# Attention with its scores turned: softmax weights stationary, row sums from columns of ones, casts shared between three engines

## The chip, the cores and the metric

The kernel runs on one core of a Trainium2 chip, in one launch. The metric is the device time of that launch in microseconds (us); less is better. Four compute engines with queues of their own take part: TensorE (PE; its weight loads are listed apart as PEld), VectorE (DVE), ScalarE (ACT) and GpSimd (POOL); SyncE (SP) issues the DMAs. Each engine works through its instructions in order and waits on semaphores for the others.

## What is computed

One layer of three blocks on 256 tokens of width 512, each added to a residual: cross attention over 4096 context rows and the 256 tokens themselves, a state-space block, and a mixture of 32 experts (6 used per token) with a shared expert. The change touches the first. Cut to what matters:

```
q = rope(rms_norm(x_norm @ wq))            # 16 heads of 128, 256 queries
k = [rms_norm(ctx @ wk_ctx), rope(rms_norm(x_norm @ wk))]   # 4 kv heads, 4096 + 256 keys
v = [ctx @ wv_ctx, x_norm @ wv]
s = q @ k.T / sqrt(128)                    # the last 256 keys are causal
w = softmax(s, axis=keys)
x = x + (w @ v).reshape(256, 2048) @ wo
```

Four heads share one kv head. Everything is float32. The kernel splits an operand into a high part (a cast to fp32r) and a low part (the rest) and sums three products: high by high, high by low, low by high.

## The kernel before, in words

The context is projected first (`project`, to about 234 us), K and V tiles with their high and low parts go to DRAM (`k_spill`, `v_spill`), and come back for one kv head at a time as `kT` (2 x 4352 keys) and `vN`. Then the attention stage runs head by head, in 17 steps a head (`NPAIR`; one step is 256 keys). The step numbers, the order of score chunks and their banks come from `Plan`: a score chunk is 128 queries by 512 keys, and scores are made one head ahead of the weights.

- `score` (L577): the queries (`qT`) are stationary and 512 keys of `kT` move, three products a chunk. `evict` (L1033, L1037, VectorE) writes the chunk to `scores` in SBUF and takes its row maximum; `maximum` makes `neg_max`.
- `exponential` (L1545, ScalarE): exp of 1024 keys for 128 queries with the row's maximum as bias; the row sums come along (`sums`), are inverted (L1052) and spread over partitions (`spread_sums`, L645).
- `turn_weights` (L593, TensorE): four transposes a step bring the weights to keys by queries in one of three banks. ScalarE casts them to the high part in the ring `pT` of four tiles (L1574), VectorE subtracts it for the low part (L1114).
- `weigh` (L616, L618), three steps behind (`LAG`): V is stationary and the weights move; 512 columns hold high and low parts side by side, then 256 columns for V's low part: four products a step. The output comes out as head width by queries, in two halves that `finish_head` adds and scales (L1060 to L1064, VectorE), casts (L1551, ScalarE) and splits (L1823, GpSimd).
- After the last head the output projection: 2 x 16 x 3 products of 512 columns (L673). While it runs, `w_xa` and `w_z` for the next block are loaded (issued by SyncE once the last value product is done), `w_xa` is split, VectorE adds the residual (L1133) and normalises (L937, `un`), and TensorE goes on with `w_z` (L686).

GpSimd's splits stand elsewhere: L1828 (`wo_lo`) at the end of the attention. L847, L849 and L741 are products of the later blocks, L493 a helper for products of several of them.

## Time and profile before

| | us |
|---|---|
| median of 3 runs | 1041.34 |
| lowest, highest | 1040.83, 1042.22 |
| the profiled execution, first to last instruction | 1040.1 |
| TensorE busy in it | 1034.4 |
| VectorE, ScalarE, GpSimd busy | 780.6, 610.6, 182.9 |

The profile is of one execution. Its span leaves out what lies around the instructions, so it stands 1.2 us under the median. Busy times of TensorE are modelled for pipelined matmuls: what a matmul costs is read from start to start. An instruction of VectorE or ScalarE overlaps the next by up to 0.1 us.

### The profile page before, as it was taken

How to read it: one execution, taken by the hardware profiler on the slowest of the kernel's cores; microseconds unless marked ns; L12 is line 12 of the kernel's file. 1: busy time of each engine (PE TensorE's matmuls, PEld its weight loads, DVE VectorE, ACT ScalarE, POOL GpSimd, SP SyncE). 2: the span in 40 equal slices, each digit the busy share in tenths (PEclk: the TensorE clock that was granted, in tenths of full speed). 3: DMA queues.
4: the chain of work that ended last, by engine and by line, in shares of the span. 5: the costliest groups of instructions: out<-in, count | busy, mean ns of one | idle time of the engine just before them, and what ended most of it. 6: DMA issues, size and time to landing. Idle time of an engine off the chain costs nothing.

```text
span 1040.1 us, 15687 instructions
## 1 busy us (share of the span) xinstructions
PE 1034.4 (99%) x5837; PEld 890.9 (86%) x5837; DVE 780.6 (75%) x1674; ACT 610.6 (59%) x1106; POOL 182.9 (18%) x200
## 2 busy tenths in 40 slices
PE   9999999999999999999999999999999999999998
PEld 8888888888888888888888888889887988888887
DVE  6856777649777777777877777877669977777775
ACT  5434343335765566665556665569469566666664
POOL 4544434330000000000000000002201132222221
...
GB/s 278 231 183 292 205 243 187 130 317 317 11 1 163 56 127 1 2 172 82 92 1 1 172 122 56 1 1 184 202 163 1 152 295 224 191 184 191 192 162 21
DMA packets 64299, 145.76 MB, mean 140 GB/s; under 512 B 3904, under 2 KB 42720, under 8 KB 62688
## 3 DMA queue, kind: packets, MB, share of 16 engines
...
q8 instruction: 46, 0.75, 0.3%
...
## 4 chain that ended last, share of the span: by engine, by line
PE 97%; DVE 2%; ACT 1%; DMA 1%; issue 0%; SPq 0%
PE bank L511 17%; PE bank L577 17%; PE bank L493 12%; PE bank L616 12%; PE bank L593 11%; PE bank L877 9%; PE bank L618 6%; PE bank L879 4%; PE bank L673 2%; PE bank L686 1%; PE bank L520 1%; DVE scores L1033 1%; PE bank L741 1%; DMA w_ctx_raw<-in_w_ctx 1%; PE bank L847 1%; PE bank L545 0%
## 5 line engine op out<-in xcount | busy, mean ns | idle before, releaser
L1114 DVE TENSOR_TENSOR pT<-bank,pT 128x512 fp32r<-128x512 f32 x272 | 184.8, 689 | 101.8 <-ACT pT L1574 100.0
L1574 ACT CAST pT<-bank 128x512 fp32r<-128x512 f32 x272 | 156.0, 593 | 141.9 <-PE bank L593 138.8
L616 PE MATMUL bank<-pT,vN 128*128 128x512 f32 (+1 forms) x544 | 225.7, 422 | 0.0
L577 PE MATMUL bank<-kT,qT_hi 128*128 128x512 f32 (+2 forms) x576 | 214.4, 391 | 0.7 <-DVE scores L1033 0.7
L1033 DVE TENSOR_SCALAR_CACHE_REDUCE scores<-bank 128x512 f32<-128x512 f32 x256 | 172.6, 686 | 1.6
L593 PE MATMUL bank<-ident,scores 128*128 128x128 f32 x1072 | 161.3, 272 | 0.1
L1545 ACT ACTIVATE scores<-scores,neg_max 128x1024 f32<-128x1024 f32 (+2 forms) x128 | 154.0, 1204 | 6.2 <-DVE neg_max L1045 6.2
L618 PE MATMUL bank<-pT,vN 128*128 128x256 f32 (+1 forms) x544 | 152.5, 280 | 0.0
L511 PE MATMUL bank<-w_ctx_hi,ctx_hl 128*128 128x512 f32 x512 | 144.5, 394 | 0.4 <-ACT w_ctx_hi L1511 0.4
L877 PE MATMUL bank<-fT_parts,e_hl 128*128 128x512 f32 x392 | 139.9, 394 | 0.0
L593 PEld LDWEIGHTS bank<-ident,scores 128*128 128x128 f32 x1072 | 127.1, 140 | 11.5 <-DVE pT L1114 0.6
L577 PEld LDWEIGHTS bank<-kT,qT_hi 128*128 128x128 f32 x576 | 108.3, 189 | 16.3 <-DVE scores L1033 1.2
L618 PEld LDWEIGHTS bank<-pT,vN 128*128 128x128 f32 x544 | 102.6, 189 | 15.6
L511 PEld LDWEIGHTS bank<-w_ctx_hi,ctx_hl 128*128 128x128 f32 x512 | 94.9, 188 | 19.9 <-ACT w_ctx_hi L1511 0.9
L879 PE MATMUL bank<-fT_parts,e_hl 128*128 128x256 f32 x392 | 110.1, 281 | 0.0
L577 PE MATMUL bank<-kT,qT_lo 128*128 128x512 f32 (+2 forms) x288 | 109.8, 381 | 0.0
L616 PEld LDWEIGHTS bank<-pT,vN 128*128 128x128 f32 x544 | 103.1, 190 | 3.8
L1692 ACT CAST e_hl<-e_raw 128x1536 fp32r<-128x1536 f32 x51 | 75.5, 1483 | 38.5 <-PE bank L493 38.5
L1823 POOL TENSOR_TENSOR outT<-head_out,outT 128x256 fp32r<-128x256 f32 x16 | 11.8, 739 | 475.1 <-ACT outT L1551 475.1
L1463 ACT ACTIVATE k_stage<-bank,k_w 128x512 fp32r<-128x512 f32 x32 | 22.1, 690 | 119.6 <-PE bank L520 119.6
L877 PEld LDWEIGHTS bank<-fT_parts,e_hl 128*128 128x128 f32 x392 | 73.5, 188 | 17.7 <-DVE e_hl L1266 0.4
L1266 DVE TENSOR_TENSOR e_hl<-e_raw,e_hl 128x1536 fp32r<-128x1536 f32 x49 | 85.9, 1753 | 0.0
...
## 6 DMA issues: line engine op xcount, KB each, us to landing
...
k_spill<-k_stage SPq DMA_DIRECT2D x16, 1024.0 KB, 5.6
v_spill<-v_stage SPq DMA_DIRECT2D x16, 1024.0 KB, 8.2
vN<-v_spill SPq DMA_DIRECT2D x16, 1024.0 KB, 5.5
kT<-k_spill SPq DMA_DIRECT2D x15, 1024.0 KB, 5.5
...
w_raw<-in_w_qkv SPq DMA_DIRECT2D x6, 1024.0 KB, 5.0
wo_sb<-in_wo SPq DMA_DIRECT2D x4, 1024.0 KB, 7.7
```

Source lines behind the costliest of these rows:

```text
L493: done = e.matmul(dst, lhs(a), rhs(w), start=first and m == 0, stop=last and m == 2)
L511: done = e.matmul(bank[2 * j + z][:, :], ctx_hl[z][:, a, k, :], w_ctx[w][:, k, j, :], start=m < 2, stop=m >= len(order) - 2)
L577: done = e.matmul(bank[b][:, 0:n], qT[a][:, h, qt * P:(qt + 1) * P], kT[:, w, lo:lo + n], start=m == 0, stop=m == 2)
L593: done = e.transpose(bank[tb][:, i * P:(i + 1) * P], s_buf[2 * z + qt][:, kt * P:(kt + 1) * P], ident[:, :])
L616: e.matmul(halves[:, :, q0:L], vN[:, 0, kt, :], ring[:, :, i * L + q0:(i + 1) * L], start=kt == 0, stop=False)
L618: done = e.matmul(halves[:, 0, q0:L], vN[:, 1, kt, :], ring[:, 0, i * L + q0:(i + 1) * L], start=False, stop=kt == KTILES - 2)
L877: e.matmul(bank[b][:, :].rearrange("p (x t) -> p x t", x=2), w[:, 0, m, k * P:(k + 1) * P], fT_parts[:, :, k, :], start=k == 0, stop=False)
L879: done = e.matmul(bank[b][:, 0:L], w[:, 1, m, k * P:(k + 1) * P], fT_parts[:, 0, k, :], start=False, stop=k == KD - 1)
L1033: e.tensor_scalar(s_buf[row][:, lo:lo + CH], bank[b][:, 0:CH], 1.0, None, ALU.mult, ALU.max, accum_out=chunk_max[row][:, c:c + 1]).then_in ...
L1114: e.tensor_tensor(ring[:, 1, :], bank[tb][:, :], ring[:, 0, :], ALU.subtract).then_inc(p_lo, 1)
L1545: e.activation(s_buf[row][:, lo:hi], s_buf[row][:, lo:hi], ACT.Exp, bias=neg_max[row][:, 0:1], scale=SCALE, accum_out=sums[z][:, qt, i:i + ...
L1574: e.copy(ring[:, 0, :], bank[tb][:, :]).then_inc(p_hi, 1)
```

## The change

The attention stage is written anew; the stages before and behind keep their instructions. A step is still 256 keys of one head, 17 a head, and the projection of the context runs on as before.

- *Scores turned.* Keys (128 of `kT`) are stationary and 256 queries move: six products a step, keys on partitions. So the weights need no transposes.
- *Maxima.* They now run over partitions. ScalarE copies each step's scores to SBUF (`take_scores`), VectorE keeps a running maximum over steps (`running_max`), folds it (`fold_max`), TensorE transposes it, VectorE reduces (`reduce_rows`), TensorE spreads it back over partitions (`spread_max`), and VectorE subtracts it from the scores in SBUF, 1024 columns at a time (`subtract_max`). ScalarE's exponentials carry no bias and no sums.
- *High and low parts.* The weights lie in SBUF. 12 of a head's 17 high parts are cast by ScalarE and 5 by VectorE (`HI_ON_DVE`), in the last 25 steps all by ScalarE; every low part is GpSimd's, in the last 25 steps every other one VectorE's.
- *Values.* The weights are stationary, 128 queries at a time, and V moves: 12 products a step of 130, 128 and 130 columns. `vH` has two columns of ones behind the 128 of the head, whose products are the row sums; `finish_head` scales by their reciprocal, and two transposes turn the output (`turn_out`).
- *Order.* Scores run 25 steps ahead (`LEAD`), values 3 behind the casts (`LAG`). 15 heads of one half of the output projection stand between the last value steps, and six of the other half ahead of the last head's transposes.

The core of the diff:

```diff
+LEAD = NG + 8
 LAG = 3
+SUB_AHEAD, EXP_AHEAD = 4, 2
+HI_ON_POOL = ()
+HI_ON_DVE = (1, 4, 7, 10, 13)
+WO_STEP = 252
+WO_PRODUCTS = 254
...
+            def score(s):
...
+                if s >= len(SCORE_BANKS):
+                    wait_score_bank(pe, s - len(SCORE_BANKS))
...
+                    for m, (a, w) in enumerate(PRODUCTS):
+                        done = e.matmul(dst, kT[:, w, kt * P:(kt + 1) * P], qT[a][:, h, q0:L], start=m == 0, stop=m == 2)
...
+            def weigh(n):
...
+                wait_lo(pe, n)
...
+                        e.matmul(bank[b][:, out:out + HV], ring[:, 0, at:at + P], vH[:, kt, :], start=kt == 0 and qt == 0, stop=False)
+                        yield
+                        e.matmul(bank[b][:, out:out + HD], ring[:, 0, at:at + P], vL[:, kt, :], start=False, stop=False)
+                        yield
+                        done = e.matmul(bank[b][:, out:out + HV], ring[:, 1, at:at + P], vH[:, kt, :], start=False, stop=kt == KTILES - 1)
...
-                    done = e.transpose(bank[tb][:, i * P:(i + 1) * P], s_buf[2 * z + qt][:, kt * P:(kt + 1) * P], ident[:, :])
...
+            for s in range(NH * NG + LEAD + LAG + 1):
...
+                n = s - LEAD
+                in_turns(score(s), weigh(n - LAG))
+                h, k = divmod(s - NG, NG)
+                if h in range(NH):
+                    if k == 1:
+                        turn_max(h)
+                    if k == 3:
+                        spread_max(h)
+                h, k = divmod(n - NG, NG)
+                if k == LAG + 1 and h in range(H15):
+                    turn_out(h)
+                if WO_PRODUCTS <= n < WO_PRODUCTS + H15:
+                    project_out(0, n - WO_PRODUCTS)
+
+            for h in range(6):
+                project_out(1, h)
+            turn_out(H15)
+            project_out(0, H15)
+            for h in range(6, NH):
+                if h == H15 - 1:
+                    pe.wait_ge(ln_out, 3)
+                    wait_score_bank_at_end(pe, 6)
+                    turn_rows(2, 0, un)
+                project_out(1, h)
...
+                    e.tensor_tensor(run_max[:, :], src[:, :], run_max[:, :], ALU.max).then_inc(maxed, 1)
...
+                    e.tensor_tensor(rows, rows, top.unsqueeze(1).to_broadcast([P, 4, L]), ALU.subtract).then_inc(subbed, 1)
...
+                e.tensor_copy(pT[n % NPT][:, 0, 0:width(g)], weights_of(n)).then_inc(p_hi["dve"], 1)
...
+            for s in range(NH * NG + LEAD):
+                n = s - LEAD
...
+                if n in plan.hi["act"]:
+                    high_of_weights(n)
+                take_scores(s)
+                for h, j in quads_at(n + EXP_AHEAD):
+                    exponential(h, j)
...
+                e.tensor_tensor(ring[:, 1], weights_of(n), ring[:, 0], ALU.subtract).then_inc(p_lo["pool"], 1)
...
-                e.dma_start(vN[:, :, lo:hi, :].bitcast(F32).rearrange("p l t d -> p l (t d)"),
-                            v_spill[g][:, :, lo:hi, :].rearrange("l p t d -> p l (t d)")).then_inc(v_in[i], 16)
+                for part, dst in enumerate((vH[:, lo:hi, 0:HD], vL[:, lo:hi, :])):
+                    e.dma_start(dst.bitcast(F32), v_spill[g, part][:, lo:hi, :]).then_inc(v_in[i], 16)
```

TensorE, in the last head of before, where no scores are left: transposes, then the value products of an earlier step (`bank` is a PSUM bank, the number behind a name its buffer).

```order
L593 MATMUL bank<-ident,scores_116 128x128 [waits p_lo]
L593 MATMUL bank<-ident,scores_117 128x128
L593 MATMUL bank<-ident,scores_116 128x128
L593 MATMUL bank<-ident,scores_117 128x128
L616 MATMUL bank<-pT_119,vN 128x512
L618 MATMUL bank<-pT_119,vN 128x256
L616 MATMUL bank<-pT_119,vN 128x512
L618 MATMUL bank<-pT_119,vN 128x256
L593 MATMUL bank<-ident,scores_116 128x128 [waits p_lo]
```

TensorE in the middle of a head after, the first 12 of a step's 18 products (operands are printed moving or stationary in either order; `pT` and `kT` are stationary here).

```order
L598 MATMUL bank<-qT_hi,kT 128x256 [waits maxed]
L619 MATMUL bank<-vH,pT_117 128x130 [waits p_lo_pool]
L621 MATMUL bank<-vL,pT_117 128x128
L598 MATMUL bank<-qT_hi,kT 128x256
L623 MATMUL bank<-vH,pT_117 128x130
L619 MATMUL bank<-vH,pT_117 128x130
L598 MATMUL bank<-qT_lo,kT 128x256
L621 MATMUL bank<-vL,pT_117 128x128
L623 MATMUL bank<-vH,pT_117 128x130
L598 MATMUL bank<-qT_hi,kT 128x256
L619 MATMUL bank<-vH,pT_117 128x130
L621 MATMUL bank<-vL,pT_117 128x128
```

The transposes are gone, and between two score products of 256 columns stand two value products of 128 or 130.

VectorE in the middle of a head, before: low parts of the weights and evictions in turns.

```order
L1114 TENSOR_TENSOR pT_119<-bank,pT_119 128x512 [waits p_hi]
L1033 TENSOR_SCALAR scores_117,chunk_max_125<-bank 128x512 [waits scored]
L1114 TENSOR_TENSOR pT_120<-bank,pT_120 128x512 [waits p_hi]
L1033 TENSOR_SCALAR scores_117,chunk_max_125<-bank 128x512 [waits scored] x2
L1114 TENSOR_TENSOR pT_121<-bank,pT_121 128x512 [waits p_hi]
L1033 TENSOR_SCALAR scores_117,chunk_max_125<-bank 128x512 [waits scored]
L1114 TENSOR_TENSOR pT_118<-bank,pT_118 128x512 [waits p_hi]
L1033 TENSOR_SCALAR scores_117,chunk_max_125<-bank 128x512 [waits scored]
```

VectorE after, around the fourth step of a head (L1065 running maximum, L1108 and L1112 the head's end, L1085 subtraction, L1096 cast).

```order
L1065 TENSOR_TENSOR run_max<-bank,run_max 128x512 [waits maxed,taken,scored]
L1108 RECIPROCAL rden_125<-bank 128x2 [waits pv]
L1112 TENSOR_TENSOR head_out_129<-bank,rden_125 128x256 [waits out_turned,ho]
L1065 TENSOR_TENSOR run_max<-bank,run_max 128x512 [waits maxed,taken,scored]
L1085 TENSOR_TENSOR weights_115<-weights_115,bank 128x1024
L1096 CAST pT_119<-weights_115 128x512 [waits pv,expd]
L1065 TENSOR_TENSOR run_max<-bank,run_max 128x512 [waits maxed,taken,scored]
L1116 TENSOR_TENSOR outT_127<-bank,outT_126 128x256 [waits oT_hi]
```

The low parts have left VectorE; a cast of this step stands behind a maximum, which waits for the scores of a group 25 steps ahead, and behind a subtraction.

GpSimd in the same place, after: one low part a step; before, it had one instruction a head there (L1823).

```order
L1887 TENSOR_TENSOR pT_117<-weights_116,pT_117 128x512 [waits pv,p_hi_act]
L1887 TENSOR_TENSOR pT_118<-weights_116,pT_118 128x512 [waits pv,p_hi_dve]
L1887 TENSOR_TENSOR pT_119<-weights_116,pT_119 128x512 [waits pv,p_hi_act]
L1887 TENSOR_TENSOR pT_120<-weights_116,pT_120 128x512 [waits pv,p_hi_act]
L1887 TENSOR_TENSOR pT_117<-weights_116,pT_117 128x512 [waits pv,p_hi_dve]
```

TensorE at the end of the attention, before: last value products, then the whole output projection.

```order
L616 MATMUL bank<-pT_121,vN 128x2x128 [waits p_lo]
L618 MATMUL bank<-pT_121,vN 128x128
L616 MATMUL bank<-pT_121,vN 128x512
L618 MATMUL bank<-pT_121,vN 128x256
L673 MATMUL bank<-wo_hi,outT_142 128x512 [waits oT_lo,wo_lo_dve,maxed]
L673 MATMUL bank<-wo_lo,outT_142 128x512
L673 MATMUL bank<-wo_hi,outT_143 128x512
L673 MATMUL bank<-wo_hi,outT_142 128x512 [waits oT_lo,wo_lo_pool]
```

TensorE there after. 45 products of the projection stand further up, between the value steps, and 51 follow.

```order
L619 MATMUL bank<-vH,pT_120 128x130
L621 MATMUL bank<-vL,pT_120 128x128
L623 MATMUL bank<-vH,pT_120 128x130
L671 MATMUL bank<-wo_hi,outT_126 128x512
L671 MATMUL bank<-wo_lo,outT_126 128x512
L671 MATMUL bank<-wo_hi,outT_127 128x512
L671 MATMUL bank<-wo_hi,outT_126 128x512
L671 MATMUL bank<-wo_lo,outT_126 128x512
```

## Rows read from the trace of the kernel before

**Rows 1.** Page: span; engine busy us (share) xinstructions; chain that ended last, by engine.
```profile
span 1040.1 us, 15687 instructions
...
PE 1034.4 (99%) x5837; PEld 890.9 (86%) x5837; DVE 780.6 (75%) x1674; ACT 610.6 (59%) x1106; POOL 182.9 (18%) x200
...
PE 97%; DVE 2%; ACT 1%; DMA 1%; issue 0%; SPq 0%
```

**Rows 2.** Stretches view, all engines, inside attention: busy us (xinstructions), clock, DMA share, GB/s.
```profile
300.00:650.00 350.00, 350.00 (x2152) 310.52 (x2151) 269.54 (x696) 219.10 (x397) 8.13 (x11) 1.00 0.23 78
```

**Rows 3.** Timeline, TensorE (start us, us, engine line op names form): attention's first and last products, w_z's.
```profile
234.37 0.71 PE L577 MATMUL bank<-kT,qT_hi 128*128 128x512 f32 x2
...
734.78 0.28 PE L618 MATMUL bank<-pT,vN 128*128 128x256 f32 x1
...
757.71 1.88 PE L686 MATMUL bank<-w_z,uT 128*128 128x512 f32 x4
```

**Rows 4.** Chain of waits in order of time (start us, us, engine, tile, line xcount).
```profile
752.29 5.58 PE bank L673 x24
...
766.87 14.29 PE bank L493 x120
...
804.79 3.52 PE bank L741 x32
```

**Rows 5.** Timeline, TensorE, 256 and 128 columns in turns.
```profile
818.23 0.33 PE L847 MATMUL bank<-fT_parts,e_hl 128*128 128x256 f32 x1
818.39 0.22 PE L849 MATMUL bank<-fT_parts,e_hl 128*128 128x128 f32 x1
818.46 0.33 PE L847 MATMUL bank<-fT_parts,e_hl 128*128 128x256 f32 x1
...
819.82 0.33 PE L847 MATMUL bank<-fT_parts,e_hl 128*128 128x256 f32 x1
```

**Rows 6.** Timeline, TensorE, a value step without scores in the last head.
```profile
713.40 0.60 PE L593 MATMUL bank<-ident,scores 128*128 128x128 f32 x4
...
714.54 0.60 PE L593 MATMUL bank<-ident,scores 128*128 128x128 f32 x4
```

**Rows 7.** Groups by line and form (busy us, mean ns | idle before).
```profile
L593 PE MATMUL bank<-ident,scores 128*128 128x128 f32 x1072 | 161.3, 272 | 0.1
```

**Rows 8.** Timeline, ScalarE: exponential, two casts from PSUM, three from SBUF.
```profile
710.33 1.17 ACT L1545 ACTIVATE scores<-scores,neg_max 128x1024 f32<-128x1024 f32 x1
...
713.56 1.10 ACT L1574 CAST pT<-bank 128x512 fp32r<-128x512 f32 x2
...
736.84 1.66 ACT L1556 CAST wo_hi<-wo_sb 128x512 fp32r<-128x512 f32 x3
```

**Rows 9.** Timeline, VectorE (evictions, splits) and GpSimd (splits).
```profile
243.79 0.68 DVE L1033 TENSOR_SCALAR_CACHE_REDUCE scores<-bank 128x512 f32<-128x512 f32 x1
...
244.40 0.69 DVE L1033 TENSOR_SCALAR_CACHE_REDUCE scores<-bank 128x512 f32<-128x512 f32 x1
...
720.92 1.29 POOL L1828 TENSOR_TENSOR wo_lo<-wo_sb,wo_hi 128x512 fp32r<-128x512 f32 x1 [0.79 <-ACT wo_hi L1556]
...
737.71 3.00 POOL L1828 TENSOR_TENSOR wo_lo<-wo_sb,wo_hi 128x512 fp32r<-128x512 f32 x2
...
739.59 2.20 DVE L1129 TENSOR_TENSOR w_xb_lo<-w_xb,wx_hi 128x1024 fp32r<-128x1024 f32 x1
744.00 4.63 DVE L1129 TENSOR_TENSOR w_xa_lo<-w_xa,wx_hi 128x1024 fp32r<-128x1024 f32 x4 [2.20 <-ACT wx_hi L1595]
```

**Rows 10.** Timeline, VectorE behind the attention: residual and normalised rows.
```profile
748.54 0.68 DVE L1133 TENSOR_TENSOR x_sb<-x_sb,bank 128x512 f32<-128x512 f32 x1
...
751.03 0.55 DVE L937 TENSOR_SCALAR un<-x_sb,moments,rstd 128x512 f32<-128x512 f32 x1 [0.67 <-POOL rstd L1787]
```

**Rows 11.** Timeline, VectorE: last instruction of the key stage.
```profile
238.04 0.69 DVE L964 TENSOR_TENSOR k_normed<-bank,k_rs 128x512 f32<-128x512 f32 x1
```

**Rows 12.** Page, DMA issues: KB each, median us to landing.
```profile
vN<-v_spill SPq DMA_DIRECT2D x16, 1024.0 KB, 5.5
```

751 lines of the change are left out of this document (374 added, 377 removed).

## The prediction

> **What bounds the kernel now.** I read the page's busy shares and the chain that ended last first, then the timeline of TensorE inside the attention stage, then those of the engines beside it. TensorE is busy 1034.4 of 1040.1 us and holds 97% of the chain [rows 1]; between 300 and 650 us it has no idle time at all, while VectorE is busy 269.5 and ScalarE 219.1 of 350 us, GpSimd 8.1 us, and the granted clock is 1.00, its 2.4 GHz level [rows 2]. So a wait on another engine is not what costs time; the cost of the matmuls, start to start, is. The attention stage runs from 234.37 us to 735.06 us (734.78 + 0.28, the end of the last value product) [rows 3]: 500.7 us.
>
> What the reader must see in the rows of TensorE is the spacing, not the duration (durations overlap). A 512-column product takes 0.233 us (24 in 5.58 us), a 256-column one 0.119 us (120 in 14.29 us), and a 64-column one still 0.110 us (32 in 3.52 us) [rows 4]. Where 256 and 128 columns alternate, seven pairs take 819.82 - 818.23 = 1.59 us, 0.227 us a pair; were the streams alone to count, 384 columns would take 0.227 x 384/512 of a 512-column price, 0.175 us [rows 4, 5]. So small products have a floor near 0.110 us, that of the weight load that each one brings along. A value step without scores lasts 714.54 - 713.40 = 1.14 us: 2 x (0.233 + 0.119) = 0.70 for four value products, and 0.44 for four transposes, 0.110 each [rows 4, 6]. Check of these prices on the kernel before, per head: scores 48 x 0.233 + 3 x 0.119 + 3 x 0.110 = 11.9; values 34 x (0.233 + 0.119) - 0.13 = 11.8; transposes of the weights 67 x 0.110 = 7.4; spreading the sums 0.2. That is 31.3 us, 501 us for 16 heads, against 500.7 in the trace. The prices hold.
>
> **What the change removes and adds on TensorE.** Removed: 1072 transposes [rows 7], 16 x 7.4 = 118 us, and the four value products of a step. The scores keep their columns but come as 256-column products: two 256s (0.238) stand for one 512 (0.233). The values turn round: the weights are stationary and the values move, so a step has 12 products of 128 or 130 columns. Their streams are no longer than before (1552 columns against 1536), but each brings a load: 12 x 0.110 = 1.32 us where 0.70 + 0.44 = 1.14 us stood. The diff shows where twelve come from: the high part meets vH and vL in two products with the same stationary tile, and the output projection of before has the same pattern (outT high with wo_hi, then wo_lo), with no product cheaper for it: 24 in 5.58 us [rows 4].
> Per head: 17 x 18 = 306 products less 3 unseen and with 3 score products halved: 99 of 256 columns, 105 + 99 small ones. 99 pairs x 0.227 = 22.5, 105 x 0.110 = 11.6, together **34.0 us**, 2.00 us a step. For 16 heads 544.4 us. Around it: 94 transposes for maxima and outputs x 0.110 = 10.3; the last keys' four, 0.4; and 15 of the 32 output-projection groups now run inside the tail, 15 x 3 x 0.233 = 10.5. Stream up to the last value product: 565.6 us.
>
> A page speaks against that floor. The Trainium skill, "TensorE: Matmul & The Clock Gate", section "Back-to-back issue gap", gives about 81 ns a product for a sustained stream of load and matmul with 128 columns; the same page, section "LDWEIGHTS (loading the stationary operand)", gives columns over 1.2 GHz, 107 ns. The trace agrees with the second (0.110 us); by the first, which no row here shows, a step would take about 1.7 us, and that is a rival below.
>
> **The other engines: does one of them pass 34.0 us a head?** ScalarE: 16 copies of scores at 0.50 (two casts from PSUM end after 1.08), 12 casts at 0.53 (three in 1.66), 8 exponentials of 1024 at 1.05 (1.17, of which 0.1 lies under the next), a short one and the output: 16 x 0.50 + 12 x 0.53 + 8 x 1.05 + 0.7 = 23.5 us [rows 8]. GpSimd, nearly idle before, gets the low part of every step: 17 x 1.29 = 21.9 us [rows 9]. VectorE: 15 running maxima, each waiting for its predecessor, at 0.69 + 0.04 = 0.73; the masked group 1.3 (three instructions of 384, 256 and 128 columns, an estimate from 0.69 for 512); folding and reducing 0.8; 8 subtractions of 1024 columns at 1.16 (four splits in 4.63) and two short ones 0.6 [rows 9]; the head's end 1.0; and 5 casts, for which the trace has no row: at most 0.69, the two-input size, at least half of 0.55, and taken as 0.55, the row of one input and 512 columns [rows 10]. That is 11.0 + 1.3 + 0.8 + 9.9 + 1.0 + 2.8 = 26.8 us. All lie under TensorE; it stays the bound, and this work is hidden in the mean.
>
> **Where it is not hidden.** (a) *VectorE's casts.* A cast of step n stands in VectorE's queue behind the running maximum of the score group s = n + 25, and in 3 of 5 cases (10, 13, 4) behind a subtraction too. From the start of TensorE's step s: the last score product, 16th of the 18, starts at 15 x 0.111 = 1.67 and is done at 1.95; ScalarE's copy to 2.57; maximum issued 2.60; subtraction 3.2 to 4.4; cast to 4.9; GpSimd 1.29, to 6.2. TensorE wants the result after three steps and one product, 6.1. Late by 0.1, and one load is then bare: 0.25 us. 14 heads x 3 + 1 = 43 such casts x 0.25 = 11 us; between nothing (a fast cast) and 0.5 each, 21 us. The other casts have a second to spare each, and ScalarE's casts more. (b) *Lead-in.* Steps 0 to 27 hold scores only, 0.71 us each; VectorE enters at 238.7 (238.04 + 0.69) [rows 11] and must do 22 maxima (16.1), the masked group (1.3), the last keys' rest (0.75), fold and reduce (0.8) and two subtractions (2.4) before TensorE may write the bank of step 28: 260.1 us. TensorE alone would be there at 234.4 + 19.9 + 1.1 = 255.4. **5 us**, between 2 and 9. In the kernel before an eviction took 0.61 us (243.79 to 244.40) [rows 9] for 0.70 us of products, and nothing was lost.
> (c) *After the last value product.* Before, TensorE took 757.71 - 735.06 = 22.65 us from there to the first product with w_z, all of it output projection [rows 3]. Its cover was long enough for w_xa's loads and splits, which the change leaves where they are: they wait for the last value product, and VectorE adds the residual (748.54) and has the normalised rows at 751.58, 16.5 us after it [rows 10]. Now only 12.1 us of projection is left, so TensorE waits: 16.5 + 0.44 for four transposes + 1.4 for two heads = 18.4 us. Against 22.65 that gives back 4.3, of the 10.5 us moved forward; 6 us are lost.
> (d) K and V tiles are requested at the same points of a head as before and have over 12 steps (24 us) to land, where 5.5 us were enough [rows 12]. The values' high half is now written in shorter pieces; at double the time it still lands early: nothing.
>
> **Sum.** 565.6 + 11 + 5 = 581.6, less 500.7, is +80.9; less 4.3, +76.6. Behind that the programs are the same. The profiled execution would be 1040.1 + 76.6 = 1116.7 us, and the median lies 1.2 us above the span: **1118 us**.
>
> **Rivals.** *The loads hide* (the other side, faster). If a small product cost only its stream, as the 0.07 us from a 128-column start to the next might suggest [rows 5], TensorE would need 17 x (6 x 0.119 + 12 x 0.06) = 24.4 us a head, VectorE's 26.8 would bound, and against the 505 us of before (500.7 + 4.3) stand 16 x 26.8 + 21.2 + 5 = 455: -50, 991 us. It decides from 0.090 us a small product: then a head takes 99 x 0.117 + 204 x 0.090 = 30 us, and the change is even. For it: a queue that loads ahead. Against it: the pairs at 0.227 and 64 columns at 0.110 [rows 4, 5]. 4%. By the 81 ns of the Trainium skill's page just named a head would take 28 us and the kernel about 1012 us; no row shows such spacing.
> *VectorE becomes the bound through GpSimd.* GpSimd now works two thirds of the time, and a VectorE instruction that reads two SBUF tiles stretches beside it: 2.20 us at 739.59, under GpSimd's 3.00, against 4.63/4 = 1.2 when alone [rows 9]. Casts, fold and masked maxima are 8 such a head; blocked by a whole 1.29 each, VectorE needs 26.8 + 10.3 = 37.1 us a head against TensorE's 34.7 (34.0 and six transposes), and the time is 1118 + 16 x 2.4 - 11 = 1145 us. It decides from 1.0 us lost each. 12%. The Trainium skill, "SBUF — State Buffer", section "Who interferes with whom", calls the shared pair an exclusive lock; maxima and subtractions have one input in PSUM and stand outside it, which leaves only the 8 named.
> *Nothing stalls.* A fast cast and a short lead-in: 565.6 + 2 - 505 = +63, 1104 us. Part of the forecast's own range.
> *A clock that falls*, since streams fill only half of TensorE's time: over 1200 us. Stretches of small products show 1.00. 2%.
>
> **How the numbers follow.** Forecast (TensorE bound by loads, small stalls) 80%: 1098 to 1135. VectorE 12%, 1135 to 1155; faster 4%; far slower (the clock, or an unseen wait in every step) 4%. The range 1096 to 1146 leaves out under 2 in 10. What a measurement can tell from no change is 0.2%, 2 us: faster 4%, same 1%, slower 95%.
>
> **What would show it.** Right: 18 products a step in 2.00 us, small ones 0.110 apart, no L593 transposes of weights, TensorE over 95% busy and the heads 34.7 to 35.5 us apart; short idle times before the step after a VectorE cast, released by GpSimd; a wait of 6 us before the transposes of un. Wrong: spacing under 0.09 us; VectorE busy all through a head with TensorE waiting for running maxima; a granted clock under 1.00.

## The result, and the profile after it

| kernel | time, us | span, us | granted clock of the span |
|---|---|---|---|
| before, four executions | 1040.8 to 1042.2 | 1040.1 | 1.00 |
| changed, two executions | 1166.2, 1166.6 | 1164.5, 1164.9 | 0.96 |
| changed, two executions | 1575.3 (profiled), 1598.4 | 1573.5, 1596.7 | 0.687, 0.676 |

The times of the changed kernel are of two kinds, and that is the result: what parts them is the granted clock of TensorE. The comparison uses the lower kind, 1.120 times the kernel before (1.118 to 1.122). The forecast was 1118 us, with 1146 as its upper end.

The profile after is of an execution of 1575 us. First the page: the span, TensorE's busy time, its busy share and its granted clock in 40 slices, and the chain by engine.

```profile
span 1573.5 us, 20080 instructions
...
PE 1556.4 (99%) x7725; PEld 1466.7 (93%) x7725; DVE 793.9 (50%) x1304; ACT 684.5 (43%) x1153; POOL 494.3 (31%) x445
...
PE   9999998999999999999999999999999989999999
...
PEclk9999999555555555555555555555555699999999
...
PE 97%; DVE 1%; DMA 1%; ACT 0%; issue 0%; POOL 0%; SPq 0%; DVEq 0%
```

Beside [rows 1] nothing looks amiss but the clock: TensorE is 99% busy and holds 97% of the chain. The granted clock reads 5, the 1.2 GHz level, in 24 slices. The stretches view (us; TensorE busy, its weight loads, VectorE, ScalarE, GpSimd, each with its count; clock; DMA share; GB/s) shows where it falls, stays and returns:

```profile
262.00:266.00 4.00, 2.61 (x19) 2.30 (x19) 3.87 (x7) 3.99 (x7) 1.33 (x2) 1.00 1.01 300
266.00:270.00 4.00, 3.70 (x26) 3.70 (x27) 2.23 (x4) 1.73 (x4) 2.74 (x3) 0.81 0.04 13
270.00:274.00 4.00, 4.00 (x21) 4.00 (x21) 1.83 (x3) 1.46 (x3) 2.78 (x3) 0.50 0.00 0
300.00:1200.00 900.00, 900.00 (x4238) 900.00 (x4236) 333.89 (x519) 328.17 (x524) 289.62 (x232) 0.50 0.10 31
1240.00:1244.00 4.00, 4.00 (x18) 3.81 (x17) 1.57 (x5) 1.79 (x4) 0.65 (x1) 0.50 0.02 4
1244.00:1248.00 4.00, 4.00 (x29) 3.75 (x29) 2.52 (x5) 1.71 (x4) 1.87 (x2) 0.91 0.00 0
```

At 0.50 the stream is the same, only slower: 900 us without a gap, where [rows 2] has 350, the other engines a third busy. The price of a product rises almost twofold. Timeline of TensorE, at 1.00 and at 0.50:

```profile
262.63 0.34 PE L598 MATMUL bank<-qT_hi,kT 128*128 128x256 f32 x1
...
262.97 0.33 PE L598 MATMUL bank<-qT_lo,kT 128*128 128x256 f32 x1
...
600.24 0.52 PE L598 MATMUL bank<-qT_hi,kT 128*128 128x256 f32 x1
...
600.88 0.52 PE L598 MATMUL bank<-qT_hi,kT 128*128 128x256 f32 x1
```

From one 256-column product to the next three products start (the 256-column one and two value products): 262.97 - 262.63 = 0.34 us at 1.00 (the prediction had 0.337), 600.88 - 600.24 = 0.64 us at 0.50. So 0.113 and 0.213 us a product: the floor of small products in [rows 4, 5] moves with the clock.

Now the last thing that TensorE did before the fall. Timelines of TensorE, VectorE and GpSimd:

```profile
266.30 0.33 PE L619 MATMUL bank<-vH,pT 128*128 128x130 f32 x1 [1.64 <-POOL pT L1887]
```

```profile
262.74 1.21 DVE L1085 TENSOR_TENSOR weights<-weights,bank 128x1024 f32<-128x1024 f32 x1
263.87 0.69 DVE L1065 TENSOR_TENSOR run_max<-bank,run_max 128x512 f32<-128x512 f32 x1
264.47 0.42 DVE L1096 CAST pT<-weights 128x512 fp32r<-128x512 f32 x1
```

```profile
261.02 1.28 POOL L1887 TENSOR_TENSOR pT<-weights,pT 128x512 fp32r<-128x512 f32 x1 [22.45 <-ACT pT L1611]
264.97 3.77 POOL L1887 TENSOR_TENSOR pT<-weights,pT 128x512 fp32r<-128x512 f32 x3 [2.67 <-DVE pT L1096]
```

The first value products stand at 262.35 us. Two microseconds on, TensorE waits 1.64 us for GpSimd's low part of step 1, GpSimd had waited for VectorE's cast (264.47), and that cast stood behind a subtraction and a running maximum. It is the only cast of the attention for which TensorE waits so. Some two us after the wait the clock is 0.50, and the waits in the lead-in before it (0.3 to 1.2 us) had not moved it. It comes back at 1244.7 us. In between one head takes 65.66 us (transposes of head_out at 464.74 and 530.40).

**What the fall costs.** From 268.5 to 1244.7 us, 976 us are spent at 0.50. A head at 1.00 takes 35.43 us (shown below). 976 x (1 - 35.43/65.66) = 449 us, and 1573.5 - 449 = 1124 us would be left. In the two executions near 1166 us a mean clock of 0.96 means some 93 us at 0.50, and 93 x 0.46 = 43 us; that leaves 1122. Both are near the forecast span of 1116.7 us. The experiments had to show that this reckoning is right, and what makes the clock fall and stay.

### The profile page after: what moved, and what is told of

Same layout as the page of the kernel before. It is cut to its first block, busy times and chain, and to the rows that moved or that the text cites. A ratio compares the mean times of both kernels' runs of the same rounds, so it can differ in the third digit from the quotient of the medians.

```text
span 1573.5 us, 20080 instructions
## 1 busy us (share of the span) xinstructions
PE 1556.4 (99%) x7725; PEld 1466.7 (93%) x7725; DVE 793.9 (50%) x1304; ACT 684.5 (43%) x1153; POOL 494.3 (31%) x445
## 4 chain that ended last, share of the span: by engine, by line
PE 97%; DVE 1%; DMA 1%; ACT 0%; issue 0%; POOL 0%; SPq 0%; DVEq 0%
PE bank L598 29%; PE bank L524 11%; PE bank L623 11%; PE bank L621 11%; PE bank L619 11%; PE bank L506 8%; PE bank L905 6%; PE bank L907 3%; PE bank L671 1%; PE bank L713 1%; PE bank L533 1%; DVE run_max L1065 1%; DMA w_xa<-in_w_in 0%; PE bank L642 0%; PE bank L769 0%; PE bank L650 0%
## 5 line engine op out<-in xcount | busy, mean ns | idle before, releaser
L1887 POOL TENSOR_TENSOR pT<-weights,pT 128x512 fp32r<-128x512 f32 (+1 forms) x259 | 323.6, 1266 | 694.1 <-DVE pT L1096 532.0
L598 PE MATMUL bank<-qT_hi,kT 128*128 128x256 f32 (+1 forms) x1088 | 526.2, 494 | 2.9 <-DVE run_max L1065 1.7
L1065 DVE TENSOR_TENSOR run_max<-bank,run_max 128x512 f32<-128x512 f32 x224 | 154.9, 691 | 480.5 <-ACT weights L1601 364.1
L619 PE MATMUL bank<-vH,pT 128*128 128x130 f32 x1072 | 384.9, 359 | 1.6 <-POOL pT L1887 1.6
L623 PE MATMUL bank<-vH,pT 128*128 128x130 f32 x1072 | 386.3, 360 | 0.0
L621 PE MATMUL bank<-vL,pT 128*128 128x128 f32 x1072 | 386.2, 360 | 0.0
L619 PEld LDWEIGHTS bank<-vH,pT 128*128 128x128 f32 x1072 | 346.1, 323 | 2.9 <-POOL pT L1887 1.8
L621 PEld LDWEIGHTS bank<-vL,pT 128*128 128x128 f32 x1072 | 346.2, 323 | 1.0
L623 PEld LDWEIGHTS bank<-vH,pT 128*128 128x128 f32 x1072 | 346.3, 323 | 0.0
L598 PEld LDWEIGHTS bank<-qT_hi,kT 128*128 128x128 f32 x1088 | 341.0, 317 | 4.3 <-DVE run_max L1065 2.5
L598 PE MATMUL bank<-qT_lo,kT 128*128 128x256 f32 (+1 forms) x544 | 267.6, 492 | 0.0
L598 PEld LDWEIGHTS bank<-qT_lo,kT 128*128 128x128 f32 x544 | 172.4, 317 | 0.0
L1085 DVE TENSOR_TENSOR weights<-weights,bank 128x1024 f32<-128x1024 f32 x128 | 154.9, 1210 | 3.9 <-PE bank L650 3.9
```

Of the source, the lines that this page charges most:

```text
L598: done = e.matmul(dst, kT[:, w, kt * P:(kt + 1) * P], qT[a][:, h, q0:L], start=m == 0, stop=m == 2)
L619: e.matmul(bank[b][:, out:out + HV], ring[:, 0, at:at + P], vH[:, kt, :], start=kt == 0 and qt == 0, stop=False)
L621: e.matmul(bank[b][:, out:out + HD], ring[:, 0, at:at + P], vL[:, kt, :], start=False, stop=False)
L623: done = e.matmul(bank[b][:, out:out + HV], ring[:, 1, at:at + P], vH[:, kt, :], start=False, stop=kt == KTILES - 1)
L1065: e.tensor_tensor(run_max[:, :], src[:, :], run_max[:, :], ALU.max).then_inc(maxed, 1)
L1085: e.tensor_tensor(rows, rows, top.unsqueeze(1).to_broadcast([P, 4, L]), ALU.subtract).then_inc(subbed, 1)
```

## Experiments: is it the stream, or the wait?

Theory A: the short products alone let the clock fall. Theory B: the waits of the lead-in (the steps with scores only, before the first value product) do. Each kernel below was executed four or six times, and one of its executions was traced. The edits are shown shortened.

**The same kernel again.**

> The changed kernel once more, unaltered, for the spread of its times and for a trace in which the clock is high most of the time. The one trace so far (span 1573.5 us) has a granted clock of 0.50 from 270 to 1244 us, while TensorE is busy without a gap; its products stand 0.213 us apart there and 0.113 us apart before and after. Both theories (A: the stream of short products, each behind its own weight load, lets the clock fall; B: the waits of TensorE in the lead-in, steps 0 to 27, let it fall, and it then stays down) expect times of two kinds again, near 1166 and near 1575 to 1598 us, with little between. In an execution near 1166 us the mean clock is 0.96: I expect some 93 us (8% of 1165) at 0.50, and a step of 18 products in 2.03 us in all the rest. At 0.50 a step lasts 3.84 us, so 93 us there cost 93 x (1 - 2.03/3.84) = 44 us, and 1166 - 44 = 1122 us would be left for the kernel at full clock.

1165.3 us once, 1577.0 to 1598.6 us five times (clock 0.676 to 0.687). The profiled execution, 1598.0 us, was again of the long kind, with the same wait of 1.64 us (it ends at 265.97 us) and the fall behind it. Here the clock stayed at 0.50 until 1298 us, not 1244.7: that is what parts 1598 from 1577. No trace of an execution near 1166 us exists, so where its 93 us at 0.50 lie was not seen.

**Value products of 256 columns.**

```diff
-e.matmul(bank[b][:, out:out + HV], ring[:, 0, at:at + P], vH[:, kt, :], ...)
+e.matmul(dst, ring[:, 0, at:at + P], vH[:, two, 0:HD], ...)   # two key tiles, 256 columns
```

> The value products move 256 columns instead of 128 or 130, over two key tiles at once, into 256 columns of the bank; so the row sums are left out and the output is another. Loads, number of products, waits and everything on the other engines stay. By the spacing of 256-column products, 0.119 us, a step lasts 18 x 0.119 = 2.14 us instead of 2.03, 28 to 30 us more in all. Theory A (the clock falls because short products behind their own loads leave the streaming part of TensorE idle): granted clock 1.00 in every execution, all times near 1122 + 30 = 1152 us, below the 1166 us of the changed kernel although more is streamed. Theory B (waits in the lead-in): those waits are the same, so the clock falls as before and the times are of two kinds, near 1195 and above 1550 us.

1147.1 to 1148.1 us. Waits of TensorE, then the stretch in which the changed kernel falls, then the attention:

```profile
PE bank L620 <- POOL pT L1888: 1.6, 1, 1.6
```

```profile
262.00:266.00 4.00, 2.45 (x20) 2.24 (x19) 4.00 (x6) 3.63 (x7) 1.43 (x2) 1.00 0.90 268
266.00:270.00 4.00, 4.00 (x34) 4.00 (x35) 2.15 (x4) 2.00 (x3) 2.35 (x2) 1.00 0.03 8
300.00:700.00 400.00, 400.00 (x3368) 399.99 (x3368) 277.67 (x415) 259.49 (x414) 236.32 (x187) 1.00 0.20 65
```

The wait is there, 1.55 us long, and the clock stays at 1.00 (row sums and so the output are others in this kernel). More is streamed than in the changed kernel, and the time is lower than its best. Even a wait of 1.00 us in the last head (794.8 us) moves nothing here. Theory B alone falls.

**The lead-in filled.**

```diff
-for m, (a, w) in enumerate(PRODUCTS):
+twice = s < LEAD + LAG and i == 0
+for m, (a, w) in enumerate(PRODUCTS + PRODUCTS + PRODUCTS if twice else PRODUCTS):
```

> In steps 0 to 27, the lead-in in which TensorE has only scores, the three products of a step's first key tile are issued three times, the last of which leaves the result; so TensorE has 1.42 us of work a step there instead of 0.71, which covers its waits for running maxima. All else is the changed kernel. The lead-in takes 28 x 1.42 = 40 us instead of 28, +12 us. Theory B (the waits in the lead-in make the clock fall): granted clock 1.00 throughout, 1122 + 12 = 1134 us in every execution. Theory A (the short products of the steps themselves): the clock falls after the first value steps as before, times near 1178 and near 1590 us.

1157.1 to 1159.1 us, and 1176.3 once. The clock is 1.00 from 220 to 788 us, through 500 us of the very stream that the long executions ran at 0.50: theory A alone falls too. It falls at 789 us, right behind a wait of 1.31 us for both_max, in the last head's steps, which have value products only:

```profile
300.00:780.00 480.00, 479.75 (x4188) 477.29 (x4186) 345.13 (x514) 323.25 (x518) 288.44 (x230) 1.00 0.18 57
780.00:790.00 10.00, 8.69 (x76) 8.55 (x76) 8.41 (x13) 6.35 (x10) 7.34 (x6) 0.98 0.40 138
790.00:800.00 10.00, 10.00 (x50) 10.00 (x49) 5.33 (x8) 4.21 (x7) 2.55 (x2) 0.50 0.83 338
```

```profile
789.24 0.46 PE L643 MATMUL bank<-ident,both_max 128*128 128x128 f32 x2 [1.31 <-DVE both_max L1072]
```

**No casts on VectorE.**

```diff
-HI_ON_DVE = (1, 4, 7, 10, 13)
+HI_ON_DVE = ()
```

> The five casts of a head that VectorE makes go back to ScalarE, nothing else is changed. The prediction put their price at 11 us (0 to 21), as loads left bare behind late low parts. At full clock I expect 11 us less than the changed kernel, 1155 us against 1166; if the casts were covered, 1166. ScalarE has 23.5 + 5 x 0.53 = 26.2 us a head and stays under TensorE's 34. Theory A and B both expect times of two kinds here too, near 1155 to 1166 and above 1550 us; a third theory (C: the late weights, small waits in each head, pull the clock down) expects 1.00 and about 1111 us in all executions.

1149.5 to 1152.4 us. No wait for GpSimd, no fall at 266 us, though the lead-in has all its waits. But there are new ones inside the attention, 14 of 0.62 us and one of 1.06 us in the last head, 9.7 us together. The 14 leave the clock at 1.00; during the one of 1.06 us, at 781 us, it falls:

```profile
PE bank L642 <- DVE both_max L1071: 9.7, 15, 1.1
```

```profile
262.00:266.00 4.00, 4.00 (x36) 4.00 (x37) 3.87 (x5) 4.00 (x8) 3.01 (x3) 1.00 0.88 263
266.00:270.00 4.00, 4.00 (x38) 4.00 (x37) 3.20 (x4) 3.42 (x6) 3.60 (x4) 1.00 0.03 6
```

So a further theory, **D**: a wait of one to two us *inside* the stream of short products lets the clock fall, and the stream does not bring it back.

## Experiments: the wait as the cause

**One wait put in by hand**, in head 8 of the kernel with the filled lead-in.

```diff
+if (h, g) == (8, GAP_AT):        # GAP_AT = 1
+    pe.wait_ge(ho, 2 * h)
```

> The kernel with the filled lead-in (three times the products of a step's first key tile in steps 0 to 27), and in it one wait of TensorE put in by hand: before the second value step of head 8 it waits until VectorE has finished head 7, which comes some 2 to 3 us later by VectorE's queue. It stands in the middle of the attention stage, where K and V loads are light. Theory D (a wait of TensorE of one to two us amid the short products lets the clock fall, and the stream of short products, 63% of TensorE's time in columns, does not bring it back): granted clock 1.00 up to this wait, 0.50 from it to the end of the value steps, 8.9 heads at 17 x 3.84 instead of 17 x 2.04 us: +270 us, 1158 + 270 less the 20 us lost at the end anyway, about 1410 us. Theory A (the short products alone) has no place for a change here: 1160 us with the fall at 790 us only. Rival E (the fall comes where the DMA queues are full, as at 266 and at 787 us, with 0.93 to 1.00 of their time): no fall at this wait, 1161 us.

1348.9, 1374.2 and 1374.6 us; once 1180.7. The wait was 1.87 us at 563.78, and the clock is 0.54 in the stretch from 564 to 568 us, 0.50 until the output projection. Three of four: the wait makes a fall likely, not sure. The DMA queues were at 0.92 just then, so rival E (full queues) was open, and so was the last head:

**The last head's transposes later**, in the kernel without casts on VectorE.

```diff
-if k == 1:
+if k == (2 if h == H15 else 1):
     turn_max(h)
```

> VectorE's casts go to ScalarE as in the run before, and for the last head alone the transposes of the maxima are issued one step later (and their spreading one step later), so that TensorE does not wait 1.06 us for VectorE at 781 us. The loads of w_z and others that fill the DMA queues from 780 us on stay. Theory D: no fall at 782 us, the clock is 1.00 up to the wait for the last rows; the 40 us at 0.50 in the kernel without VectorE's casts cost 40 x (1 - 1.35/2.56) = 19 us, so 1150.3 - 19 = 1131 us. Rival E (full DMA queues): fall as before, 1150 us.

1142.6 to 1143.8 us, and 1166.2 once. The wait at 781 us is gone, and the clock stays 1.00 there, with the queues at 1.01. It falls ten us later instead, at about 792 us, behind a new wait of 1.93 us for wo_lo. The edit shifted the wait, and the fall went with it; the expected 1131 us did not come.

**The wait in head 9, where the DMA queues are idle**, again with the filled lead-in.

```diff
+if (h, g) == (9, 1):
+    pe.wait_ge(ho, 2 * h)
```

> As the kernel with the filled lead-in and one wait put in by hand, but the wait stands in head 9 instead of head 8, near 598 us, where the DMA queues are under 0.02 busy for 45 us around (in head 8 they were at 0.92). Theory D: the fall comes at this wait in some or most executions (in head 8 in 3 of 4), and lasts to the end of the value steps: 5.9 x 2 = some 25 to 30 us less than the runs with the wait in head 8, since one head of 34.9 us at full clock would take 65 at half: 1349 - 31 = 1318, 1374 - 31 = 1343 us. Rival E (full DMA queues are needed): no fall at 598 us in any execution, 1161 us.

1318.3, 1318.5, 1340.6 and 1340.9 us, the expected 1318 and 1343. The DMA share is 0.00 to 0.02 at the fall, which lasts 388 us, from 599 to 987. Rival E falls.

```profile
590.00:594.00 4.00, 4.00 (x37) 4.00 (x37) 2.79 (x4) 2.65 (x4) 0.93 (x1) 1.00 0.00 0
594.00:598.00 4.00, 2.41 (x22) 2.21 (x20) 2.92 (x6) 2.54 (x4) 3.77 (x3) 1.00 0.00 0
598.00:602.00 4.00, 3.72 (x20) 3.75 (x20) 0.14 (x1) 0.50 (x2) 0.00 (x0) 0.58 0.02 4
602.00:606.00 4.00, 4.00 (x21) 4.00 (x20) 2.15 (x3) 1.87 (x4) 1.59 (x2) 0.50 0.00 0
```

**One cast moved**, that of step 1 of head 0.

```diff
-"dve" if n < tail and g in HI_ON_DVE else "act"
+"dve" if 1 < n < tail and g in HI_ON_DVE else "act"
```

> The changed kernel, in which one single cast, that of the high part of step 1 of head 0, goes from VectorE to ScalarE; the other 74 of VectorE's casts stay. In the slow traces it is this step's low part for which TensorE waits 1.64 us at 264.3 us, the last wait before the clock falls. Theory D (a wait amid the short products lets the clock fall, the stream of short products keeps it down): this wait goes, and with it the long fall, in every or nearly every execution; times 1150 to 1166 us, a mean clock of 0.96 to 0.98, and a fall only near 782 us. Theory A (short products alone) and F (VectorE's casts in general, through late weights in every head): times of two kinds as before, 1166 and 1577 to 1598 us.

1141.7 to 1145.3 us in all four. One instruction of 0.42 us, moved to another engine, takes away 434 us of the usual time (medians 1577.5 and 1143.6). The changed kernel's best time lies 23 us above this one, and that is mostly something else: 1.6 us are the wait, and some 20 fit a longer fall in the last head (below), with 93 us at 0.50 where this kernel has 48. Its clock is 1.00 until 777 us; then it falls during the last head's wait (1.31 us), for 38 us. VectorE's other casts are worth keeping: this kernel is 6.7 us faster than the one without them, as the waits for both_max, from 230 to 900 us, come to 2.7 us instead of 10.8.

**No fall at the end either.** In addition 12 products of 512 columns, overwritten later, in front of the last head's transposes.

```diff
+if k == 1 and h == H15:
+    wait_score_bank(pe, NH * NG - len(SCORE_BANKS))
+    for _ in range(12):
+        e.matmul(bank[SCORE_BANKS[0]][:, :], vH[:, 0, 0:HD], vH[:, 0:4, 0:HD], start=True, stop=True)
     turn_max(h)
```

> The cast of step 1 of head 0 on ScalarE as before, and in front of the transposes of the last head's maxima 12 products of 512 columns whose results are overwritten (12 x 0.233 = 2.8 us), so that TensorE does not wait 1.31 us there; all else is the changed kernel. Theory D: granted clock 1.00 from the start to the wait for the last rows, 16 heads, and the time is that of the changed kernel at full clock: 1143.6, less 40 us at 0.50 x (1 - 1.35/2.56) = 19, plus 2.8 - 1.3 = 1.5, 1126 us; the forecast of 1118 came without the head's both_max waits and with 2.00 us a step. If the short products without scores lose the clock by themselves (value steps of 12 products of 128 columns, 48% in columns), the fall comes all the same and the time is near 1146 us.

1127.0 to 1127.8 us against 1126 expected. The clock is 1.00 up to the wait for `un`. This is the changed kernel as the prediction had reckoned it, 2.9 us of fill included (12 products from 774.68 to 777.57 us).

## Experiments: why it does not come back

**64 columns a value product**, in the kernel without casts on VectorE. It asks whether a shorter wait is enough where the products carry fewer columns; half of the values and the row sums are left out.

```diff
-e.matmul(bank[b][:, out:out + HV], ring[:, 0, at:at + P], vH[:, kt, :], ...)
+e.matmul(bank[b][:, out:out + 64], ring[:, 0, at:at + P], vH[:, kt, 0:64], ...)
```

> Without VectorE's casts, and each value product moves 64 columns instead of 128 or 130, into the first 64 columns; so half of the values and the row sums are left out, and the output is another. All loads, waits and other engines' work stay. If the load sets the pace (0.110 us with 64 columns as with 128, as the prediction took it), a step lasts 1.98 instead of 2.03 us: about 1140 us at the same clock, against 1150. The columns then fill 2304 of 4750 possible ones of a step, 48% against 63%. [...]

1348.9, 1407.3, 1467.3 and 1526.4 us: four falls, by the times in four different heads. In the trace the pace at 1.00 is that of the changed kernel (three products in 0.34 us), and six waits of 0.64 to 0.66 us do nothing before the one at 495 us, behind which the next product is at half pace. With 128 columns fourteen waits of 0.62 us did nothing. So fewer columns make a shorter wait enough, and chance has a part.

```profile
494.05 0.37 PE L598 MATMUL bank<-qT_lo,kT 128*128 128x256 f32 x1
...
495.19 0.66 PE L642 MATMUL bank<-ident,both_max 128*128 128x128 f32 x2 [0.64 <-DVE both_max L1071]
495.50 0.56 PE L598 MATMUL bank<-qT_hi,kT 128*128 128x256 f32 x1
495.86 0.26 PE L619 MATMUL bank<-vH,pT 128*128 128x64 f32 x1
```

**48 products of 512 columns in the middle** of the changed kernel.

```diff
+if s == 5 * NG + 8:
+    for _ in range(48):
+        e.matmul(bank[b][:, :], kT[:, 0, piece * PIECE:piece * PIECE + P], kT[:, 0, piece * PIECE:piece * PIECE + 512], start=True, stop=True)
```

> The changed kernel with 48 products of 512 columns (results overwritten) put in once, before the scores of step 8 of head 5, when TensorE is in step 65 of the 244 that hold scores and values. Theory D with its second half (at half clock the stream of short products does not bring the clock back, more columns would): in executions in which it fell at 266 us, the clock comes back to 1.00 with the burst, at about 266 + 65 x 3.84 = 516 us, and stays there until the end of the scores: 65 x 1.8 = 117 us lost instead of some 410 to 430, 1166 + 117 + 11 = 1294 us in place of 1577 to 1598. In executions in which it did not fall, 1177 us. If the clock cannot come back amid the stage at all (it is held down for a time of its own): 1588 to 1610 us.

Twice 1156 us, four times 1253.3 to 1270.5 (expected 1294). The burst starts at about 513 us; the stretch from 512 to 516 us has 0.77, the next 1.00, and it stays so to the last head (900 us). The clock can come back amid the stage, and it holds once it is up.

In the last head 15 value steps carry three 512-column products of the output projection each. Fourteen traces run them at 0.50, from the first on. In ten the clock is back in the sixth such step, some 21 us after the first (first at 1223.9, back at 1244.7; in the kernel with one cast moved 793.4 and 814.4). In four (the second trace of the changed kernel, 64 columns, and two kernels below) it stays at 0.50 through all 15 and comes back 3 to 5 us after the projection's products stand alone. Here is one of the four (the last of the kernels with score products in a row, below), where the first such product stands at 805.1 us:

```profile
794.00:826.00 32.00, 32.00 (x135) 30.26 (x134) 14.65 (x22) 13.20 (x21) 10.14 (x10) 0.50 0.13 50
826.00:874.00 48.00, 48.00 (x200) 45.40 (x199) 10.92 (x19) 12.50 (x19) 12.38 (x10) 0.50 0.00 0
```

Between the two traces of the changed kernel this makes 1598 us of 1575, and it would explain the step of 18 to 26 us that other kernels show too (1318 and 1341, 1157 and 1176). A fall of this length, 88 us, without the one at 266 us would also give the changed kernel's 93 us and 1166 us; an estimate, for no such execution was traced. What decides between the two lengths no run shows.

At 0.50 such a step has 3088 columns in 3.84 us, as has a step with six score products in turns, and in those the clock came back in no trace unless the burst above was put in. Four more runs vary how the products stand.

**Score products in a row**, ahead of the value products.

```diff
 for _ in scores:
-    for _ in range(2):
-        next(values, None)
+    pass
```

> The changed kernel with one change of order on TensorE: the six score products of a step stand in a row ahead of the twelve value products, instead of each between two of them. The same products, loads, columns and waits. At full clock a step takes 6 x 0.119 + 12 x 0.111 = 2.05 us, as before. If the alternation of 256 and 128 columns is what holds the clock down (products in a row stream denser for 0.7 us, as the output projection's do): the clock comes back some 20 us after a fall, times 1135 to 1170 us in all executions. If it is not: times of two kinds again, near 1166 and 1577 to 1598 us.

1137.6 to 1141.8 us four times, 1175.2 and 1176.2 us (clock 0.947, some 124 us at 0.50). No fall of hundreds of us in six, with the same products and VectorE's casts in place. But the wait for GpSimd in step 1 is shorter too, 1.20 us for 1.64, and the clock stays at 1.00 behind it in the trace. So this run does not tell a clock that falls less readily from one that comes back.

**Three products of 512 columns for the six of 256.**

```diff
-done = e.matmul(dst, kT[:, w, kt * P:(kt + 1) * P], qT[a][:, h, q0:L], ...)
+done = e.matmul(dst, kT[:, w, kt * P:(kt + 1) * P], qT[a][:, hh:hh + 2, :], ...)   # 512 columns
```

> The six score products of 256 columns of a step become three of 512 columns, over two heads' queries and the first key tile alone, so the scores and the output are others; 3 loads fewer a step, the same number of columns, the same instructions on all other engines. A step at full clock takes 3 x 0.233 + 12 x 0.111 = 2.03 us; it is then just the step of 12 value products and 3 products of the output projection in which the clock comes back after 21 us. If long products (or fewer loads) are what brings it back: no long fall in any execution, 1120 to 1150 us. If the clock came back there for another reason (the place in the program, the DMA queues): times of two kinds, above 1500 us among them.

1155.4, 1156.0, 1178.2, 1266.8, 1266.8 and 1324.9 us: at most some 447 us at 0.50 (0.831) instead of nearly a thousand. The trace, of the 1156.0 us, has a wait of 1.65 us for GpSimd and stays at 1.00 behind it. Neither of the two outcomes that I had expected: in these six executions long products, each between short ones, helped less than the rows did.

**Row and wait together**, with the filled lead-in. In the first kernel the wait came out at 0.3 us:

```diff
 for _ in scores:
-    for _ in range(2):
-        next(values, None)
+    pass
...
+if (h, g) == (9, 1):
+    pe.wait_ge(ho, 2 * h)
```

> The kernel with the filled lead-in and the wait put in by hand in head 9 (near 598 us, DMA queues idle), and in it the six score products of each step in a row ahead of the twelve value products. With the products in turns this kernel took 1318 to 1341 us, at 0.50 from 599 us to the end. If the order brings the clock back: a fall at about 598 us and a return some 20 to 80 us later, each 76 us at half clock costing 76 x (1 - 2.04/3.84) = 36 us, times 1158 to 1200 us. If the order only made the fall at the second step less likely: at 0.50 from 598 us to the end, 1318 to 1341 us.

1149.9 to 1153.2 us, and 1174.1 once; with so short a wait it tells nothing. In the second `(9, 0)` stands in place of `(9, 1)`:

> As the run with score products in a row and a wait put in by hand in head 9, but the wait for VectorE's end of head 8 stands one step earlier, between the scores and the values of step 0, and is 2 to 3 us long; the DMA queues are idle there. If the order brings the clock back: a fall behind the wait, in the steps after 596 us, and a return 20 to 80 us later; 76 us at 0.50 would cost 36 us, times 1154 to 1200 us. If it does not: 0.50 from there to the end, 1318 to 1345 us. If the row only makes the clock less ready to fall: 1.00 at the wait in all executions, 1154 us.

1155.1 to 1202.2 us. The wait was 2.32 us, the longest of all:

```profile
590.00:594.00 4.00, 3.08 (x27) 2.88 (x26) 2.85 (x4) 3.16 (x5) 2.87 (x3) 1.00 0.00 0
594.00:598.00 4.00, 2.60 (x16) 2.63 (x17) 1.19 (x3) 0.00 (x0) 0.89 (x1) 0.79 0.01 4
598.00:602.00 4.00, 4.00 (x21) 4.00 (x21) 2.16 (x3) 2.16 (x3) 0.28 (x1) 0.50 0.00 0
602.00:606.00 4.00, 4.00 (x33) 4.00 (x33) 1.17 (x3) 2.30 (x5) 3.04 (x3) 0.86 0.00 0
606.00:610.00 4.00, 4.00 (x37) 4.00 (x37) 3.45 (x6) 2.73 (x4) 1.46 (x2) 1.00 0.00 0
```

The clock falls and is back within 8 us, where with the products in turns it stayed down for 388. That is one trace. The other five executions have mean clocks of 0.939 to 0.980, some 46 to 146 us at 0.50; some 46 or more of them belong to the last head and to `un`, so the longest fall in head 9 can have been some 100 us (an estimate). The wait itself differs, 2.32 us and one step earlier for 1.87, but the stream behind it differs only in its order. So the order in which a step's products stand decides whether the clock returns soon. Why a row of 256-column products does what the same products in turns don't, no run shows.

**A candidate with the values stationary** and the weights moving again, the row sums from a product with ones as its stationary operand.

```diff
-e.matmul(bank[b][:, out:out + HV], ring[:, 0, at:at + P], vH[:, kt, :], ...)     # 12 a step
+e.matmul(halves[:, :, q0:L], vH[:, kt, :], ring[:, :, at], ...)                   # 6 a step: 512,
+e.matmul(halves[:, 0, q0:L], vL[:, kt, :], ring[:, 0, at], ...)                   # 256 and
+e.matmul(bank[SUM_BANKS[h % 2]][:, q0:L], ones_r[:, :], ring[:, 0, at], ...)      # 256 columns
```

> A candidate. The scores stay turned, so that no weights are transposed, but the values are the stationary operand again and the weights move, 512 columns (high and low) with vH and 256 with vL, per key tile; the row sums come from one 256-column product per key tile with ones as the stationary operand and the weights' high part. All casts of high parts on ScalarE. The outputs come out turned, so their transposes go too; VectorE adds the halves and divides by the sums, 4 instructions a head. A step: 6 x 0.119 for scores, 2 x 0.233 + 2 x 0.119 for values, 2 x 0.119 for the sums, 1.66 us against 2.04; 90% of TensorE's time in columns. Per head 17 x 1.66 = 28.2, with four transposes 28.6; 16 heads 458 us, lead-in 26, output projection in the tail 10.5: about 500 us up to the last value product against 581 by the prediction's sum, so near 1122 - 81 - 11 = 1030 us at most, 1014 if no waits come. Theory D: clock 1.00 in every execution, since the columns fill the time. ScalarE 26.2 and VectorE 26 us a head are just under TensorE's 28.6; if they bind, 1045 us.

1073.7 to 1075.5 us, 1.032 (1.030 to 1.033) of the kernel before, clock 1.00 up to 724 us, near the end of the attention. The expected 1014 to 1045 us did not come; the waits:

```profile
PE bank L644 <- DVE both_max L1069: 22.4, 16, 2.1
PE bank L599 <- DVE run_max L1063: 15.7, 18, 1.0
PE bank L513 <- DVE un L963: 6.3, 1, 6.3
```

```profile
400.00:700.00 300.00, 273.72 (x1949) 253.61 (x1948) 249.16 (x329) 244.57 (x403) 202.92 (x160) 1.00 0.19 61
```

TensorE now catches up with VectorE, 83% busy from 400 to 700 us, and is itself at 91% (I had only three banks left for scores). None of its waits up to 724 us brings a fall. It is 52 us faster than the best of the kernels above and still slower than the kernel before, which none of the runs beats.

## The prediction, point by point

**The clock.** It stood among the rivals, as "A clock that falls, since streams fill only half of TensorE's time", at 2%, with "Stretches of small products show 1.00" as its refutation. That is the step that failed: the sum held the clock at 1.00 throughout, and put the clock's term at nothing. The rows behind it were stretches of 3.5 us [rows 4] and the like, without a wait in them; the new stage is 500 us of them and has waits of its own. What the runs showed in its place: behind one wait of 1.64 us a long fall in 7 of the 10 executions of the changed kernel, 976 us at 0.50 and worth 449 us in the first trace; and near 1166 us some 93 us at 0.50, worth 43 of the 48 us above the forecast. The rival named half of the cause (few columns). The other half was in the prediction as well, as (a): a late low part behind a VectorE cast, though in other steps, priced at one bare load of 0.25 us. I did not put the two together. The forecast's 1146 as an upper end took in every wait at its own length and none at what it sets off. The list of signs did name it: "a granted clock under 1.00".

**Removed and added on TensorE: right, 2% low.** Rows of the kernel with the cast moved and 12 products of 512 columns put in, called the repaired kernel from here on; they answer to [rows 2, 3]:

```profile
235.55 0.49 PE L598 MATMUL bank<-qT_hi,kT 128*128 128x256 f32 x2
...
338.08 0.44 PE L659 MATMUL bank<-ident,head_out 128*128 128x128 f32 x2
...
373.51 0.44 PE L659 MATMUL bank<-ident,head_out 128*128 128x128 f32 x2
...
822.71 0.28 PE L623 MATMUL bank<-vH,pT 128*128 128x130 f32 x1
...
839.71 1.11 PE L512 MATMUL bank<-ident,un 128*128 128x128 f32 x4 [4.76 <-DVE un L969]
...
843.18 2.32 PE L717 MATMUL bank<-w_z,uT 128*128 128x512 f32 x3
```

```profile
300.00:400.00 100.00, 100.00 (x875) 99.48 (x874) 72.78 (x110) 67.44 (x109) 61.11 (x49) 1.00 0.25 78
```

Two heads' transposes of head_out are 373.51 - 338.08 = 35.43 us apart, forecast 34.0 and 0.66 for transposes. Of the 0.8 us over, some 0.4 is the spacing, 2.04 us a full step for 2.02 by the prices, and some 0.2 the transposes, 0.27 to 0.31 us a pair for 0.22; in 16 heads the 0.8 make 12 us. One slip in the prediction's working, without effect on the sum: 384 columns by stream alone are 0.233 x 384/512 = 0.175 us, where it prints 0.227 for 0.233.

The Trainium skill's 81 ns a product ("TensorE: Matmul & The Clock Gate", section "Back-to-back issue gap") does not hold for this stream: 113 ns. The same page's 107 ns for a load (section "LDWEIGHTS (loading the stationary operand)") is near at 1.00, but the page gives it without regard to the granted clock, and here the spacing rose from 113 to 213 ns at 0.50.

**(a) Casts: wrong in size and in place.** Instead of 43 stalls of 0.25 us, 11 us together, the filled lead-in shows one, of 0.2 us. A cast takes 0.42 us (assumed 0.55). There are 73 of them, so 72 besides the first, where the expectation on it said 74. The one that was late is the first, in step 1 of head 0. It is none of the 43, which are casts of steps 4, 10 and 13; the prediction had it among those with time to spare. It cost 1.64 us, since VectorE arrives there late from the lead-in.

**(b) Lead-in, 5 us:** waits of 1.17, 0.27, 0.37, 1.12, 0.31 and 0.74 make 4.0 us. Right, only that they are spread over the lead-in and not at its end.

**(c) Behind the last value product, 18.4 us:** 843.18 - 822.99 = 20.2. `un` is ready 16.7 us after it (16.5 forecast), and the wait of 6 us came as 4.76 and 1.0 for outT before it. What the sum had not is the clock, 0.75 from 840 to 850 us: the transposes of `un` and the two heads of projection took 3.5 us for 1.84. **(d)** vH lands in 4.1 us, vL in 5.0, against 5.5 in [rows 12]: nothing waited.

**The sum, at full clock.** Last value product at 822.99, first score product at 235.55: 587.4 us, less 2.9 of fill, 584.5, against 581.6 forecast: 11 us too many for casts, 1 for the lead-in, 12 too few for the heads; some 3 us more lie in parts that were not taken apart. The two large errors cancel by luck, so the total being near says little for the parts. The span is 1126.1 - 2.9 = 1123 against 1116.7.

**The other engines: right.** Per head, from the stretch 300 to 400 us above: VectorE 25.8 (26.8), ScalarE 23.9 (23.5), GpSimd 21.7 us (21.9). **VectorE through GpSimd (12%):** the head stays TensorE's. The stretching exists (both_max, 256 columns from two SBUF tiles, takes 1.44 us in the kernel without VectorE's casts, where TensorE waits for it, and 0.41 in the repaired one), but not in eight instructions a head. **The loads hide (4%):** no, 0.113 us a product.
